# One of four low one-hot blocks of the expert stage moved from the vector engine to the scalar engine

## The chip, the cores and the metric

The kernel runs on one core of a Trainium2 chip. The metric is the device time of one execution in microseconds (us). Five instruction streams run side by side and meet only at semaphores: TensorE (PE, with its weight loads shown as PEld), VectorE (DVE), ScalarE (ACT), GpSimd (POOL) and SyncE (SP). Each runs its own instructions in the order in which they are written.

## The reference, cut to what matters

The network has four layers; the first three are left alone here. The last one is a product-key expert layer over 4 x 512 tokens of 128 numbers:

```python
q = (xn @ w_q.T).reshape(b, s, 2, NH, KD).transpose(2, 0, 1, 3, 4)
sim = jnp.einsum('pbnhd,hkpd->bpnhk', q, keys_p)          # 2 sides x 8 heads x 32 keys
scores, idx = jax.lax.top_k(sim, K)                        # K = 8 on each side
all_scores = scores[0][..., :, None] + scores[1][..., None, :]
all_idx = idx[0][..., :, None] * NK + idx[1][..., None, :] # NK = 32
sc, pk = jax.lax.top_k(all_scores, K)                      # 8 experts for each head
hmid = jax.nn.sigmoid(sc) * gelu(inputs . down[indices])
out = sum(hmid * up[indices])                              # over heads and k
```

So each token picks 64 experts (8 heads x 8) out of 1024 (32 x 32), with a weight for each.

## The kernel before

The first three layers are computed in the function layers(), the expert layer in peer(). It works on 16 tiles of 128 tokens, numbered u, in 8 **pairs** p of two tiles (256 tokens). Instead of gathering rows of down and up, it computes gelu(x . down) for all 1024 experts (hid) and multiplies it by a dense matrix of weights, which it builds from one-hots. An expert's number is split into a low part (0 to 127, the number modulo 128) and a high part (8 values). For every one of the 128 lanes (one token of either tile) TensorE multiplies a one-hot of the low parts (hot_lo, 128 chosen experts of the two tokens x 128 values) with the weighted one-hot of the high parts (hot_w), in two products (high and low half of the weight). The lanes are treated in QB = 4 **blocks** of LB = 32 lanes; block q has its own PSUM bank 2 + q.

The order in a pair is written out by hand on each engine, one loop over p from -1 to 7.

- VectorE, pair p: one_hots(p), which makes in_lo, w_lo, hi_t, lo_t, hot_hi, four hot_w and the four hot_lo blocks; residual(p - 1); second_choice of tiles 2p+2 and 2p+3, which ends in rc; normal(p - 1); which_side of both tiles, which writes eq from the rc that ScalarE has cast to 16 bits; weigh(p), which writes the four mix blocks, each once TensorE has filled its bank; first_choice of tiles 2p+4 and 2p+5.
- ScalarE, pair p: decoded(p), which brings the numbers of the chosen experts from PSUM (sides_t, w_hi, w_t) and so releases one_hots(p); side_numbers of two tiles (side_f); three hidden() (gelu of hid for the next 512 tokens); for even p normed() (xn); then in turn rows_columns(2p+2) (the cast of rc), key_scores(2p+4) (the copy keysims), rows_columns(2p+3), key_scores(2p+5); then sigmoids and one more hidden().
- TensorE, pair p: decoded(p); three hidden(); gathered(p), the 256 products of hot_lo and hot_w in four blocks, each behind hot_ok and its bank's mix_ok; key_scores(2p+4) and (2p+5), of which the second waits for ScalarE's copy of the first; one hidden(); outputs(p) behind the last mix.
- GpSimd: numbers(u) behind eq, candidates(u), root(p).

Pairs 0 to 5 have work for the next 512 tokens (hidden) and key scores; pairs 6 and 7 have neither.

Of the kernel before, what the change touches and what calls it, by code (L numbers as in the profile page):

```python
# [16 lines left out]
ALU = mybir.AluOpType  # L17
# [7 lines left out]
P = 128  # L25
# [1341 lines left out]
def peer(nc, v):  # L1367
# [5 lines left out]
    QB = P // LB  # L1373
# [10 lines left out]
    with ctx:  # L1384
# [19 lines left out]
        sides_t = sb("sides_t", [P, 2, P], U32)  # L1404
        w_t, w_hi, w_lo = sb("w_t", [P, P]), sb("w_hi", [P, P], F16), sb("w_lo", [P, P], F16)
        in_lo, lo_t, hi_t = sb("in_lo", [P, P], U32), sb("lo_t", [P, P], F16), sb("hi_t", [P, P], F16)
        hot_lo = sb("hot_lo", [P, P // 2, P, 2], F16)
        hot_hi = sb("hot_hi", [P, P // 2, EH, 2], F16)
        hot_w = sb("hot_w", [P, 2, P // 2, 2, EH, 2], F16)
# [10 lines left out]
        cand_ok, best_ok, rc_ok, rc16_ok = sem("cand_ok"), sem("best_ok"), sem("rc_ok"), sem("rc16_ok")  # L1420
        eq_is, eq_ok, sig_ok = sem("eq_is"), sem("eq_ok"), sem("sig_ok")
        dec_mm, dec_ok, split_ok = sem("dec_mm"), sem("dec_ok"), sem("split_ok")
        hot_ok, g_mm, mix_ok = sem("hot_ok", QB), sem("g_mm", QB), sem("mix_ok", QB)
        out_mm, z4_ok, var_ok, rstd_ok = sem("out4_mm"), sem("z4_ok"), sem("var4_ok"), sem("rstd4_ok")
        o4_ok, stored = sem("o4_ok"), (sem("stored0", 16), sem("stored1", 16))
        own = sem("dve_own4", 0)
# [1 line left out]
        with nc.Block() as block:  # L1428
# [52 lines left out]
            @block.scalar  # L1481
            def _(act):
                def normed(b):

                    if b:
                        wait(act, ksim_mm, T * b - 1)
                    nc.scalar.activation(xn[:], v.x3t[:, N * b:N * b + N], ACT.Identity, bias=bn_shift[:],
                                         scale=v.bn_scale[:]).then_inc(xn_ok.h, 1)

                def key_scores(u):  # L1490

                    wait(act, ksim_mm, u)
                    if u >= 4:
                        wait(act, found_ok, u - 4)
                    nc.scalar.copy(keysims[:, u % 4].rearrange("p s k -> p (s k)"), bank[6][:]).then_inc(ksim_ok.h, 1)  # L1495

                def hidden(b, c):

                    if b >= 2:
                        wait(act, mix_ok, PB * (b - 1) - 1)  # L1500
                    wait(act, h_mm, b, c + 1)
                    nc.scalar.activation(hid[:, b % 2, :, c, :], bank[H_BANK(b, c)][:].rearrange("p (t l) -> p t l", t=T),  # L1502
                                         ACT.Gelu).then_inc(h_ok.h, 1)

                def side_numbers(u):

                    wait(act, found_ok, u)
                    if u >= 4:
                        wait(act, eq_ok, u - 4)
                    nc.scalar.copy(side_f[:, u % 4].rearrange("p i r h -> p i h r"),  # L1510
                                   side_i[:, u % 4].rearrange("p (i h) r -> p i h r", i=2)).then_inc(side_f_ok.h, 1)

                def rows_columns(u):

                    wait(act, rc_ok, u)
                    if u >= 2:
                        wait(act, eq_is, u - 2)
                    nc.scalar.copy(rc16[:, u % 2], rc[:, u % 2]).then_inc(rc16_ok.h, 1)  # L1518

                def sigmoids(u):  # L1520

                    wait(act, best_ok, u)
                    if u >= 2:
                        wait(act, dec_mm, u // 2 - 1)
                    nc.scalar.activation(weight[:, u % 2], best[:, u % 2], ACT.Sigmoid).then_inc(sig_ok.h, 1)

                def decoded(p):

                    wait(act, dec_mm, p)
                    if p:  # L1530
                        wait(act, split_ok, p - 1)
                        wait(act, g_mm, p - 1)
                    nc.scalar.copy(sides_t[:].rearrange("p i l -> p (i l)"), bank[1][:, 0:2 * P])
                    nc.scalar.mul(w_hi[:], bank[1][:, 2 * P:3 * P], WEIGHT_SCALE)
                    nc.scalar.copy(w_t[:], bank[1][:, 2 * P:3 * P]).then_inc(dec_ok.h, 1)

                nc.scalar.copy(ident_h[:], ident[:]).then_inc(ident_ok.h, 1)
                act.wait_ge(bn_done.h, 1)
                normed(0)
                hidden(0, 0)  # L1540
                hidden(0, 1)
                for u in (0, 1):
                    key_scores(u)
                for c in range(2, EH):
                    hidden(0, c)
                for p in range(-1, PAIRS):
                    ahead = p >= 0 and p // PB + 1 < B
                    if p >= 0:
                        decoded(p)
                    if p + 1 < PAIRS:  # L1550
                        for u in (2 * p + 2, 2 * p + 3):
                            side_numbers(u)
                    if ahead:
                        for c in HID_EARLY[p % PB]:
                            hidden(p // PB + 1, c)
                    if p >= 0 and p + 2 < PAIRS and (p + 2) % PB == 0:
                        normed((p + 2) // PB)
                    for u in (2 * p + 2, 2 * p + 3):
                        if p < 0:
                            key_scores(u + 2)  # L1560
                        if u < TILES:
                            rows_columns(u)
                        if p >= 0 and u + 2 < TILES:
                            key_scores(u + 2)
                    if p + 1 < PAIRS:
                        for u in (2 * p + 2, 2 * p + 3):
                            sigmoids(u)
                    if ahead:
                        for c in HID_LATE[p % PB]:
                            hidden(p // PB + 1, c)  # L1570

            @block.vector
            def _(dve):
# [40 lines left out]
                def one_hots(p):  # L1614

                    wait(dve, dec_ok, p)
                    if p:
                        wait(dve, g_mm, p - 1)
                    nc.vector.tensor_scalar(in_lo[:], sides_t[:, 0], IN_LO - 1, None, ALU.bitwise_and)
                    step(nc.vector.scalar_tensor_tensor(w_lo[:], w_t[:], WEIGHT_SCALE, w_hi[:], ALU.mult, ALU.subtract))  # L1620
                    nc.vector.tensor_tensor(hi_t[:], sides_t[:, 0], in_lo[:], ALU.subtract)  # L1621
                    step(nc.vector.scalar_tensor_tensor(lo_t[:], in_lo[:], float(NK), sides_t[:, 1], ALU.mult, ALU.add))
                    step(nc.vector.tensor_tensor(  # L1623
                        hot_hi[:], bc(hi_t[:].rearrange("p (j s) -> p j s", s=2).unsqueeze(2), [P, P // 2, EH, 2]),
                        bc(iota_hi4[:].unsqueeze(1), [P, P // 2, EH, 2]), ALU.is_equal))
                    for t in range(2):
                        q = slice(HK * t, HK * t + HK)
                        for i, w in enumerate((w_hi, w_lo)):
                            ins = nc.vector.tensor_tensor(  # L1629
                                hot_w[q, i, :, t], hot_hi[q],  # L1630
                                bc(w[q].rearrange("p (j s) -> p j s", s=2).unsqueeze(2), [HK, P // 2, EH, 2]),
                                ALU.mult)
                    ins.then_inc(split_ok.h, 1)
                    for q in range(QB):
                        lanes, pairs = slice(LB * q, LB * q + LB), slice(LB // 2 * q, LB // 2 * (q + 1))
                        nc.vector.tensor_tensor(  # L1636
                            hot_lo[:, pairs],
                            bc(lo_t[:, lanes].rearrange("p (j s) -> p j s", s=2).unsqueeze(2), [P, LB // 2, P, 2]),
                            bc(v.iota_lo[:].unsqueeze(1), [P, LB // 2, P, 2]), ALU.is_equal).then_inc(hot_ok.h, 1)
# [78 lines left out]
            def _(pe):  # L1718
# [37 lines left out]
                def gathered(p):  # L1756

                    for q in range(QB):
                        wait(pe, hot_ok, p, q + 1)
                        if p:  # L1760
                            wait(pe, mix_ok, p - 1, q + 1)
                        for lane in range(LB * q, LB * q + LB):
                            for i in range(2):
                                c = 2 * EH * (lane % LB)
                                ins = nc.tensor.matmul(  # L1765
                                    bank[2 + q][:, c:c + 2 * EH], hot_lo[:, lane // 2, :, lane % 2],
                                    hot_w[:, i, lane // 2, :, :, lane % 2].rearrange("p t e -> p (t e)"),
                                    start=(i == 0), stop=(i == 1))
                        ins.then_inc(g_mm.h, 1)
# [63 lines left out]
```

## Time and profile before

| | |
|---|---|
| time, median of 3 runs | 667.36 us (666.91 to 669.09) |
| profiled execution, its time | 663.84 us |
| profiled execution, its span | 662.1 us |
| VectorE busy over the span | 526.0 us, 79% |
| TensorE busy | 433.0 us, 65% |
| ScalarE busy | 199.9 us, 30% |
| GpSimd busy | 197.5 us, 30% |
| expert stage | from about 374 us to the end at 662 us |

The engines' shares are means over stages with different limits; the expert stage is read apart below. All positions in time are from the start of the span of this one profiled execution, whose own time lies 3.5 us under the median.

### The profile page before, as it was taken

The page shows a single profiled execution, that of the slowest core. Times are in us where ns is not written, and L with a number is a line of the kernel's source. Part 1 is how long each engine was busy: PE and PEld are TensorE (multiplying, and loading weights), DVE is VectorE, ACT ScalarE, POOL GpSimd, SP SyncE. Part 2 cuts the span into 40 slices and gives each one's busy share as a digit, 9 for nine tenths or more (in the row PEclk, how much of TensorE's full clock was granted, in tenths as well). Part 3 has the DMA queues.
Part 4 walks back from the last instruction along what each step waited for, and adds up shares of the span by engine and source line. Part 5 has one row for each costly group of instructions (what it writes and reads, how often), then busy time and mean ns, then how long its engine had stood idle before and what let it go on. Part 6 is the DMA issues. An engine that isn't in the chain of part 4 may idle for free. (4 is left out here: it accounts for less than half of the span.)

```text
span 662.1 us, 12046 instructions
## 1 busy us (share of the span) xinstructions
PE 433.0 (65%) x4504; PEld 308.1 (47%) x4504; DVE 526.0 (79%) x2100; ACT 199.9 (30%) x348; POOL 197.5 (30%) x185
## 2 busy tenths in 40 slices
PE   3776477775767658785276546867677767774344
PEld 2562256643655337653165214544544444544344
DVE  1668588688676977768874499999999999999783
ACT  2210264304452054521452343323232323231100
POOL 4332215703166130751256331303030303030200
PEclk9979767597865978567765685665856675756566
DMA  5500000000000000000000000000000000000000
GB/s 140 155 1 0 0 2 1 1 1 0 1 1 1 1 0 1 2 1 0 0 2 1 0 1 1 1 2 10 1 10 2 9 1 9 2 9 1 9 2 16
DMA packets 12456, 6.69 MB, mean 10 GB/s; under 512 B 3182, under 2 KB 11758, under 8 KB 12398
## 3 DMA queue, kind: packets, MB, share of 16 engines
q1 hardware_dynamic: 10622, 4.34, 2.6%
q10 hardware_dynamic: 1776, 1.58, 0.9%
q8 instruction: 35, 0.57, 0.4%
q14 instruction: 23, 0.19, 0.1%
HBM read 4.87 MB, written 1.05 MB: 9 GB/s over the span
## 5 line engine op out<-in xcount | busy, mean ns | idle before, releaser
L1765 PE MATMUL psum<-hot_w,hot_lo 128*128 128x16 f16 x2048 | 59.8, 174 | 29.7 <-DVE hot_lo L1636 29.7
L1765 PEld LDWEIGHTS psum<-hot_w,hot_lo 128*128 128x128 f16 x2048 | 57.1, 104 | 40.2 <-DVE hot_lo L1636 39.5
L1636 DVE TENSOR_TENSOR hot_lo<-lo_t,iota_lo 128x4096 f16<-128x4096 f16 x32 | 71.2, 2285 | 0.3
L1778 PE MATMUL psum<-upw,mix 128*128 128x128 f32 x256 | 45.5, 359 | 27.0 <-DVE mix L1651 27.0
L1739 PE MATMUL psum<-x3t,down_t 128*128 128x512 f32 x64 | 47.5, 850 | 22.4 <-ACT hid L1502 19.6
L1778 PEld LDWEIGHTS psum<-upw,mix 128*128 128x128 f32 x256 | 43.9, 271 | 36.3 <-DVE mix L1651 36.3
L1182 PE MATMUL psum<-q_hi,k_t 32*128 32x128 f16 x256 | 42.6, 285 | 27.5 <-DVE feat L830 18.8
L557 POOL TENSOR_TENSOR s_lo<-masked,s_hi 128x512 f16<-128x512 f32 x32 | 36.2, 1165 | 67.7 <-ACT s_hi L431 67.7
L1454 POOL TENSOR_TENSOR eq<-eq,side_f 128x1024 f16<-128x1024 f16 x16 | 33.1, 2090 | 69.1 <-DVE eq L1610 69.1
L1462 POOL TENSOR_TENSOR rstd<-rstd,minus_half 128x2 f32<-128x2 f32 x8 | 5.6, 705 | 129.0 <-DVE rstd L1668 129.0
L1182 PEld LDWEIGHTS psum<-q_hi,k_t 32*128 32x128 f16 x256 | 28.0, 125 | 32.9 <-DVE feat L830 20.9
L1182 PE MATMUL psum<-q_lo,k_t 32*128 32x128 f16 x256 | 43.3, 290 | 0.0
L1588 DVE FIND_INDEX8 side_i<-side,keysims 128x8 uint32<-128x32 f32 x256 | 41.5, 185 | 0.0
L1118 PE MATMUL psum<-we,x1t 128*128 128x512 f32 x64 | 37.4, 731 | 3.5 <-DVE z L761 3.5
L557 POOL TENSOR_TENSOR s_lo<-feat,s_hi 128x512 f16<-128x512 f32 x32 | 36.0, 1159 | 10.1 <-ACT s_hi L431 10.1
L1726 PE MATMUL psum<-keysim,xn 128*128 128x512 f32 x32 | 29.0, 1004 | 11.2 <-ACT keysims L1495 9.8
L1739 PEld LDWEIGHTS psum<-x3t,down_t 128*128 128x128 f32 x64 | 14.0, 253 | 46.2 <-ACT hid L1502 34.6
L1518 ACT CAST rc<-rc 128x128 f16<-128x128 uint32 x16 | 4.8, 298 | 100.1 <-DVE rc L1604 100.1
L761 DVE SCALAR_TENSOR_TENSOR z<-psum,wexp,z 128x128 f32<-128x128 f32 x112 | 29.6, 342 | 0.0
L1584 DVE MAX8 side<-keysims 128x8 f32<-128x32 f32 x256 | 25.2, 176 | 4.7 <-ACT keysims L1495 4.7
L1182 PEld LDWEIGHTS psum<-q_lo,k_t 32*128 32x128 f16 x256 | 28.0, 128 | 0.0
L1502 ACT ACTIVATE hid<-psum 128x512 f32<-128x512 f32 x32 | 20.6, 648 | 24.4 <-PE psum L1739 24.3
(237 smaller groups left out, 1075.4 us busy)
## 6 DMA issues: line engine op xcount, KB each, us to landing
xall<-in_L_attn_x SPq DMA_DIRECT2D x4, 256.0 KB, 4.7
out<-o SPq DMA_DIRECT2D x8, 128.0 KB, 1.8
we<-in_L_ffn_We SPq DMA_DIRECT2D x1, 512.0 KB, 4.1
downn<-in_L_ffn_down SPq DMA_DIRECT2D x1, 512.0 KB, 6.0
upw<-in_L_ffn_up SPq DMA_DIRECT2D x1, 512.0 KB, 6.8
wh<-in_L_attn_W_h SPq DMA_DIRECT2D x1, 256.0 KB, 4.2
keysn<-in_L_ffn_keys_p ACTq DMA_DIRECT2D x1, 256.0 KB, 11.7
wqkv<-in_L_attn_w_qkv ACTq DMA_DIRECT2D x1, 192.0 KB
```

Of the source, the lines that this page charges most:

```text
L557: nc.gpsimd.tensor_tensor(s_lo[:, u % 2, g, :], masked[u % 2][:, g, :], s_hi[:, u % 2, g, :], ALU.subtract).then_inc(slo_ok.h, 1)
L761: ins = nc.vector.scalar_tensor_tensor(z2[:, u, :], src, wexp[:, u, e:e + 1], (z2 if e else x1)[:, u, :], ALU.mult, ALU.add)
L1118: ins = nc.tensor.matmul(bank[Y_BANK[u] + k][:], x1t[:, P * u:P * u + P], v.we[:, 4 * k:4 * k + 4, :].rearrange("p e m -> p (e m)"), start ...
L1182: ins = nc.tensor.matmul(bank[4 + g % 2][:, P * c:P * c + P], k_t[r, u, c, :], q[r, u, c, :], start=(q is q_hi), stop=(q is q_lo))
L1454: nc.gpsimd.tensor_tensor(hit, hit, bc(side_f[:, u % 4].rearrange("p i r h -> p (i r) h").unsqueeze(3), [P, 2 * K, NH, K]), ALU.mult)\
L1584: ins = nc.vector.max(side[:, u % 4, s, :], keysims[:, u % 4, s, :])
L1588: ins = nc.vector.max_index(side_i[:, u % 4, s, :], side[:, u % 4, s, :], keysims[:, u % 4, s, :])
L1636: nc.vector.tensor_tensor(hot_lo[:, pairs], bc(lo_t[:, lanes].rearrange("p (j s) -> p j s", s=2).unsqueeze(2), [P, LB // 2, P, 2]), bc(v.i ...
L1726: nc.tensor.matmul(bank[6][:], xn[:, P * (u % T):P * (u % T) + P], v.keysim[:].rearrange("p s k -> p (s k)"), start=True, stop=True)\
L1739: nc.tensor.matmul(bank[H_BANK(b, c)][:], v.down_t[:, c, :], v.x3t[:, N * b:N * b + N], start=True, stop=True).then_inc(h_mm.h, 1)
L1765: ins = nc.tensor.matmul(bank[2 + q][:, c:c + 2 * EH], hot_lo[:, lane // 2, :, lane % 2], hot_w[:, i, lane // 2, :, :, lane % 2].rearrange ...
L1778: ins = nc.tensor.matmul(bank[0][:, P * t:P * t + P], mix[:, EH * t + e, :], v.upw[:, e, :], start=(e == 0), stop=(e == EH - 1))
```

## The change

VectorE makes three of the four hot_lo blocks of a pair. The fourth (lanes 96 to 127) is made by ScalarE in a new function last_one_hots(p). VectorE first writes lo_last, the low numbers of those 32 lanes as 32-bit floats. ScalarE then writes, for each of the 32 lanes, the distance of the numbers 0 to 127 (iota_f) from the lane's low number, |iota - lo|, with the lane's column of lo_last as the bias of an Abs instruction, and at last max(1 - distance, 0) over the whole block of 4096 columns in place. TensorE's fourth block waits for hot_last_ok.

```diff
+        lo_last, iota_f = sb("lo_last", [P, LB]), sb("iota_f", [P, P])
...
-        hot_ok, g_mm, mix_ok = sem("hot_ok", QB), sem("g_mm", QB), sem("mix_ok", QB)
+        hot_ok, g_mm, mix_ok = sem("hot_ok", QB - 1), sem("g_mm", QB), sem("mix_ok", QB)
+        lo_last_ok, far_ok, hot_last_ok = sem("lo_last_ok"), sem("far_ok"), sem("hot_last_ok")
...
+                def last_one_hots(p):
+                    pairs = slice(LB // 2 * (QB - 1), LB // 2 * QB)
+                    act.wait_ge(lo_last_ok.h, p + 1)
+                    for lane in range(LB):
+                        ins = nc.scalar.activation(hot_lo[:, LB // 2 * (QB - 1) + lane // 2, :, lane % 2], iota_f[:],
+                                                   ACT.Abs, bias=lo_last[:, lane:lane + 1], scale=-1.0)
+                    ins.then_inc(far_ok.h, 1)
+                    act.wait_ge(far_ok.h, p + 1)
+                    nc.scalar.activation(hot_lo[:, pairs], hot_lo[:, pairs], ACT.Relu, bias=1.0, scale=-1.0)\
+                        .then_inc(hot_last_ok.h, 1)
...
+                nc.scalar.copy(iota_f[:], v.iota_lo[:, :, 0])
...
                     if ahead:
                         for c in HID_EARLY[p % PB]:
                             hidden(p // PB + 1, c)
+                    if p >= 0:
+                        last_one_hots(p)
                     if p >= 0 and p + 2 < PAIRS and (p + 2) % PB == 0:
                         normed((p + 2) // PB)
...
                     nc.vector.tensor_tensor(hi_t[:], sides_t[:, 0], in_lo[:], ALU.subtract)
+                    last = slice(LB * (QB - 1), LB * QB)
+                    nc.vector.scalar_tensor_tensor(lo_last[:], in_lo[:, last], float(NK), sides_t[:, 1, last], ALU.mult,
+                                                   ALU.add).then_inc(lo_last_ok.h, 1)
...
-                    for q in range(QB):
+                    for q in range(QB - 1):
...
                     for q in range(QB):
-                        wait(pe, hot_ok, p, q + 1)
+                        if q < QB - 1:
+                            wait(pe, hot_ok, p, q + 1)
+                        else:
+                            pe.wait_ge(hot_last_ok.h, p + 1)
+                            wait(pe, split_ok, p)
```

On ScalarE the instructions of pair 1, from the three gelu of hid to the second copy of key scores, stood like this before:

```order
L1502 ACTIVATE hid<-psum 128x4x128 [waits h_mm] x3
L1518 CAST rc<-rc 128x128 [waits eq_is,rc_ok]
L1495 COPY keysims<-psum 128x512 [waits found_ok,ksim_mm]
L1518 CAST rc<-rc 128x128 [waits eq_is,rc_ok]
L1495 COPY keysims<-psum 128x512 [waits found_ok,ksim_mm]
```

and stand like this now:

```order
L1505 ACTIVATE hid<-psum 128x4x128 [waits h_mm] x3
L1546 ACTIVATE hot_lo<-iota_f,lo_last 128x128 [waits lo_last_ok]
L1546 ACTIVATE hot_lo<-iota_f,lo_last 128x128 x31
L1550 ACTIVATE hot_lo<-hot_lo 128x4096 [waits far_ok]
L1521 CAST rc<-rc 128x128 [waits eq_is,rc_ok]
L1498 COPY keysims<-psum 128x512 [waits found_ok,ksim_mm]
L1521 CAST rc<-rc 128x128 [waits eq_is,rc_ok]
L1498 COPY keysims<-psum 128x512 [waits found_ok,ksim_mm]
```

The 33 new instructions stand between the gelus and the two casts of rc. No table load is added to ScalarE's stream in any pair.

On TensorE the fourth block of gathered and the key scores behind it stood like this before (the first of the two key scores waits for xn_ok, the second for ksim_ok of the first):

```order
L1765 MATMUL psum<-hot_w,hot_lo 128x16 [waits mix_ok,hot_ok]
L1765 MATMUL psum<-hot_w,hot_lo 128x16 x63
L1726 MATMUL psum<-keysim,xn 128x512 [waits ksim_ok,xn_ok] x2
L1739 MATMUL psum<-x3t,down_t 128x512 [waits h_ok]
L1778 MATMUL psum<-upw,mix 128x128 [waits z4_ok,mix_ok]
```

and stand like this now:

```order
L1791 MATMUL psum<-hot_w,hot_lo 128x16 [waits mix_ok,split_ok,hot_last_ok]
L1791 MATMUL psum<-hot_w,hot_lo 128x16 x63
L1748 MATMUL psum<-keysim,xn 128x512 [waits ksim_ok,xn_ok] x2
L1761 MATMUL psum<-x3t,down_t 128x512 [waits h_ok]
L1804 MATMUL psum<-upw,mix 128x128 [waits z4_ok,mix_ok]
```

TensorE's order is the same; the fourth block's wait is for ScalarE instead of VectorE.

## Rows read from the trace of the kernel before

**Rows 1.** The page, part 5: the hot_lo group.

```profile
L1636 DVE TENSOR_TENSOR hot_lo<-lo_t,iota_lo 128x4096 f16<-128x4096 f16 x32 | 71.2, 2285 | 0.3
```

**Rows 2.** Busy time of the engines, pair 3 and pair 6 (windows).

```profile
500.40:533.50 33.10, 24.11 (x317) 16.03 (x317) 32.64 (x177) 8.87 (x17) 6.99 (x5) 0.64 0.02 6
599.60:632.00 32.40, 14.38 (x305) 13.81 (x305) 24.35 (x80) 3.73 (x9) 4.85 (x3) 0.58 0.02 5
```

**Rows 3.** Timeline of VectorE, first instruction of pairs 0, 1, 2, 3, 7.

```profile
402.97 0.20 DVE L1619 TENSOR_SCALAR in_lo<-sides_t 128x128 uint32<-128x128 uint32 x1
434.18 0.21 DVE L1619 TENSOR_SCALAR in_lo<-sides_t 128x128 uint32<-128x128 uint32 x1
467.38 0.23 DVE L1619 TENSOR_SCALAR in_lo<-sides_t 128x128 uint32<-128x128 uint32 x1
500.45 0.20 DVE L1619 TENSOR_SCALAR in_lo<-sides_t 128x128 uint32<-128x128 uint32 x1
632.05 0.23 DVE L1619 TENSOR_SCALAR in_lo<-sides_t 128x128 uint32<-128x128 uint32 x1 [7.71 <-ACT w_t L1535]
```

**Rows 4.** Timeline of VectorE: hot_lo and eq of pair 3, mix of 0, 3, 7.

```profile
504.76 8.90 DVE L1636 TENSOR_TENSOR hot_lo<-lo_t,iota_lo 128x4096 f16<-128x4096 f16 x4
521.50 1.28 DVE L1610 TENSOR_TENSOR eq<-rc,iota_r 128x1024 f16<-128x1024 f16 x2
...
423.39 2.47 DVE L1651 SCALAR_TENSOR_TENSOR mix<-psum,hid 128x512 f32<-128x512 f32 x4
...
522.70 2.48 DVE L1651 SCALAR_TENSOR_TENSOR mix<-psum,hid 128x512 f32<-128x512 f32 x4
...
647.95 2.48 DVE L1651 SCALAR_TENSOR_TENSOR mix<-psum,hid 128x512 f32<-128x512 f32 x4
```

**Rows 5.** Timeline of ScalarE: third hid of pairs 0 to 3, xn behind it.

```profile
410.68 0.60 ACT L1502 ACTIVATE hid<-psum 128x512 f32<-128x512 f32 x1 [2.17 <-PE psum L1739]
411.17 0.81 ACT L1487 ACTIVATE xn<-x3t,bn_shift,bn_scale 128x512 f32<-128x512 f32 x1
...
440.40 0.60 ACT L1502 ACTIVATE hid<-psum 128x512 f32<-128x512 f32 x1 [2.17 <-PE psum L1739]
...
472.13 0.60 ACT L1502 ACTIVATE hid<-psum 128x512 f32<-128x512 f32 x1 [1.28 <-PE psum L1739]
...
506.26 0.60 ACT L1502 ACTIVATE hid<-psum 128x512 f32<-128x512 f32 x1 [2.22 <-PE psum L1739]
```

**Rows 6.** Timeline of ScalarE: casts and copies of pairs 3 and 0.

```profile
518.07 0.30 ACT L1518 CAST rc<-rc 128x128 f16<-128x128 uint32 x1 [11.21 <-DVE rc L1604]
518.27 0.58 ACT L1495 COPY keysims<-psum 128x512 f32<-128x512 f32 x1
...
420.06 0.59 ACT L1495 COPY keysims<-psum 128x512 f32<-128x512 f32 x1 [0.50 <-PE psum L1726]
```

**Rows 7.** Timeline of ScalarE: gates of layer 1; w_hi, w_t, side_f.

```profile
247.89 1.25 ACT L357 ACTIVATE gate_t<-psum,bh_gate 128x512 f32<-128x512 f32 x2
...
431.07 0.28 ACT L1534 ACTIVATE w_hi<-psum 128x128 f16<-128x128 f32 x1
431.24 0.27 ACT L1535 COPY w_t<-psum 128x128 f32<-128x128 f32 x1
431.38 0.77 ACT L1510 CAST side_f<-side_i 128x128 f16<-128x128 uint32 x1
```

**Rows 8.** Groups of ScalarE by form: the gates.

```profile
L357 ACT ACTIVATE gate_t<-psum,bh_gate 128x512 f32<-128x512 f32 x8 | 5.1, 679 | 2.5 <-PE psum L1034 2.5
```

**Rows 9.** Timeline of TensorE, pair 0: fourth block, first key scores.

```profile
416.24 1.87 PE L1765 MATMUL psum<-hot_w,hot_lo 128*128 128x16 f16 x64 [0.33 <-DVE hot_lo L1636]
417.97 2.05 PE L1726 MATMUL psum<-keysim,xn 128*128 128x512 f32 x2
```

**Rows 10.** Timeline of TensorE and ScalarE: from outputs of pair 1 to decoded of pair 2.

```profile
458.97 6.62 PE L1778 MATMUL psum<-upw,mix 128*128 128x128 f32 x32 [2.49 <-DVE mix L1651]
465.42 1.06 PE L1750 MATMUL psum<-ident_h,eq 128*128 128x128 f16 x16
...
467.07 0.27 ACT L1535 COPY w_t<-psum 128x128 f32<-128x128 f32 x1
```

## The prediction

> **What bounds the kernel now.** I read the page's groups first: the 32 hot_lo blocks are the costliest VectorE group at 2285 ns each, 71.2 us [rows 1]. The busy time by stretch comes next. In pair 3 VectorE is busy 32.64 of 33.10 us, and ScalarE only 8.87 [rows 2]. So in the inner pairs VectorE is the bound, and what is taken from it comes back in full, as long as nothing it waits for gets late. In the stretch of pair 6 it is busy 24.35 of 32.40 us; it waits at the end for outputs and decoded, but these start behind its last mix, so the path still runs through it.
>
> The question is thus not the share of ScalarE but what stands behind the new block there. Two things do: the casts of rc, without which VectorE can't make eq, and the copies keysims. ScalarE runs in order, and the slots are given by the timeline. I count from the first instruction of one_hots in a pair, T: 402.97, 434.18, 467.38, 500.45 for pairs 0 to 3 [rows 3]. VectorE starts mix at T + 20.42 in pair 0 and at T + 22.25 in pair 3 [rows 3, 4].
>
> **What it removes.** Four blocks take 8.90 us, so a block is worth (8.90 - 2.285) / 3 = 2.2 us [rows 1, 4]. lo_last is new: 32 columns, a small instruction beside the 128 columns of in_lo (0.20 us) [rows 3]; I take 0.1 us, with 0 and 0.3 as the bounds, 2.4 us over 8 pairs at most. Where VectorE stays the bound, a pair gains 2.1 us.
>
> **What it adds on ScalarE.** The trace has no Abs with a column as bias on 128 columns, so its price is bounded. What counts is the distance from start to start. With no column as operand, w_hi to w_t on 128 columns from PSUM is 0.17 us [rows 7]; the cast of rc, which reads SBUF as the new instruction does, is followed after 0.20 us [rows 6]. The price of a column: two gates with a bias column take 1.25 us together and 0.679 each, so 0.57 from start to start [rows 7, 8]; hid, as wide but without one, is followed after 0.49 [rows 5]. That is 0.08 more. I take 0.20 + 0.08 = **0.28 us**, built from the nearest rows. The bounds: 0.17, if column and SBUF cost nothing, and 0.38 (0.30 of rc plus 0.08), if the instructions don't overlap.
>
> The last Abs must end before the Relu starts, 0.10 us. The Relu: 128 columns take 0.28 us [rows 7] and 512 take 0.60 [rows 5], 0.83 ns a column, so 4096 take 0.60 + 3584 x 0.83 ns = 3.58. The whole block is 32 x 0.28 + 0.10 + 3.58 = **12.64 us**.
>
> The Trainium skill gives another price for the 32 (ScalarE: Activation LUTs, section What ACT_TABLE_LOAD costs): an ACTIVATE with a column as bias takes some 280 ns + 0.833 ns a column, of which neighbours overlap by 93 ns. That is 0.294 us for 128 columns, an estimate from its figures, and would make the block 13.1 us and my result 2.7 us longer.
>
> **When it starts and ends.** In pairs 0 to 5 it stands behind the third hid. The next instruction can start 0.49 us after that one did (xn in pair 0) [rows 5]. Counted from T that is 8.20, 6.71, 5.24 and 6.30 us in pairs 0 to 3 [rows 3, 5]; pairs 2 and 3 are the shortest and longest of the last four, and I take their mean 5.77 for all four. lo_last is there long before, within 1 us of T.
>
> **What waits for it.** At the block's end TensorE may start the fourth block (0.05 for the signal, as w_t's end to in_lo in pair 2 [rows 3, 10]). Its key scores follow 1.73 us after that start [rows 9], and ScalarE's copy of them starts 2.09 us after theirs [rows 6, 9]. Only behind that copy stands the cast of rc of the pair's second tile: it starts 0.49 later (spacing as of hid), takes 0.30 [rows 6], 0.05 for the signal, then the second eq, 0.60 until mix [rows 4]. Together 5.31 us. So this is a loop through three engines: the block, TensorE's fourth block and key scores, the copy, the cast, eq. Before, the fourth hot_lo was followed by 8 us of other VectorE work before eq, which hid all of it. The normed of even pairs goes in TensorE's 1.87 us.
>
> Mix then starts at T + start of the block + 12.64 + 5.31:
> - pair 0: 8.20 + 17.95 = 26.15 instead of 20.42: 5.7 us later
> - pair 1: 6.71 + 17.95 = 24.66 instead of 22.25: 2.4 later
> - pairs 2 to 5: 5.77 + 17.95 = 23.72 instead of 22.25: 1.5 later each, 5.9
> - pair 6: no hid and no key scores. The block runs from T + 0.9 to T + 13.6, before eq at T + 21.05 - 2.1 (eq by pair 3 [rows 3, 4]). Full gain, -2.1.
> - pair 7: the block ends at 632.05 + 0.9 + 12.64 = 645.6, TensorE at 647.5 with its 1.87 [rows 3, 9]. VectorE starts mix 2.1 us earlier, at 645.85, and the fourth mix 1.8 us later, at 647.65 [rows 4]. Just hidden: -2.1.
>
> What follows mix keeps its distance: first_choice on VectorE, beside it outputs, decoded and w_t. In pair 1 outputs took 6.62 us, and w_t ended 0.04 us before in_lo started [rows 3, 10], so even slow outputs just fit. GpSimd's numbers start earlier than outputs end.
>
> **The sum.** 5.7 + 2.4 + 5.9 - 4.2 = +9.8 us on 663.84, so 673.6. The median of before is 3.5 us over its profiled execution; on it the time is **677.2 us**.
>
> **The rivals.** About 0.3%, 2 us, is what a measurement can tell from no change.
> - *Faster: the loop closes in time.* At 0.17 us an Abs the block is 9.1 us and mix comes at T + start + 14.4: pair 0 is 2.2 late, pair 1 gains 1.1, pairs 2 to 5 some 1.9 each, pairs 6 and 7 4.2, in all -10.7, 656.7 us. Each 0.01 us of the Abs is 1.9 us of the kernel, so it decides from 0.23 us downwards. For it: w_hi to w_t [rows 7]; ScalarE is idle enough. Against: the gates show that a column costs. 0.12.
> - *No change:* an Abs at 0.22 to 0.24 us, the gain of some pairs eaten by the others: 667.4. 0.06.
> - *No overlap:* at 0.38 us the block is 15.7 us, six pairs lose 3.1 more each, and in pair 7 TensorE ends 2.9 after the fourth mix could start: +31, 699 us. For it: all new instructions read the same tile and write 2-byte values between each other's. Against: the gates overlap by 0.11. 0.10.
> - *The spread write is slow:* an Abs writes every second 2-byte value. side_f also writes spread values, 16 bytes apart, and takes 0.77 us for 128 columns instead of 0.30 [rows 6, 7]. At such a price (0.75 us) the block is 27.7 us, six pairs lose 15 more, pairs 6 and 7 some 20: about 790 us. Against: hot_lo's steps are 4 bytes. 0.03. The Trainium skill (SBUF — State Buffer, section Door 1: The DMA port swizzle) says that accesses pay only where fewer than two fall in one 16-byte line; four do so here, one for side_f, whose row agrees.
> - *As forecast,* 0.69.
>
> **The numbers.** The forecast's own range is an Abs of 0.25 to 0.32 us (-5.8 to +7.7 us), and if TensorE's slower clock makes every pair's hid as late as pair 1's, another 4 x 0.94 = 3.8. That is 671 to 689, and 669 to 690 with an edge to the cases beside it; it leaves out most of the fast rival and of the two slow ones, about 2 in 10. Faster 0.12, the same 0.06, slower 0.82.
>
> **What would show it.** Right: VectorE idles before the second eq or before mix in pairs 0 to 5, most in pair 0, released by ScalarE's rc; ScalarE's Abs start every 0.28 us; mix starts 23 to 26 us after in_lo in pairs 0 to 5 and 20 in pair 6; TensorE idles before its fourth block for hot_lo from ScalarE. Wrong: no VectorE idle time there, or Abs spaced by less than 0.23; a TensorE clock so low after the longer gap that hid comes later than 7 us after in_lo; table loads ahead of the Abs.

## The result, and the profile after

| | before | after |
|---|---|---|
| median time | 667.83 us (4 runs, 666.91 to 669.09) | 683.57 us (4 runs, 681.50 to 683.97) |
| ratio | 1 | 1.0222, 95% interval 1.0197 to 1.0247 |
| span of the profiled execution | 662.1 us | 682.2 us |
| first one_hots to the end | 259.1 us | 274.2 us |

The kernel is 15.7 us slower; forecast were 9.8, in a range of 669 to 690 us. The kernel before was profiled in an execution of 663.84 us, faster than any of its four timed ones. Of the 20.1 us between the two spans 5.0 lie ahead of the first one_hots, and all of these are there before ScalarE makes iota_f (at 377.59 in the kernel after), the one instruction that the change adds in that part. I therefore compare from the first in_lo to the end: 682.2 - 408.02 = 274.2 against 662.1 - 402.97 = 259.1, 15.1 us, which agrees with the medians.

The page of the kernel after, part 5, has four groups that answer to [rows 1] or show its consequence:

```profile
L1791 PE MATMUL psum<-hot_w,hot_lo 128*128 128x16 f16 x2048 | 59.9, 174 | 69.3 <-ACT hot_lo L1550 43.2
L1546 ACT ACTIVATE hot_lo<-iota_f,lo_last 128x128 f16<-128x128 f32 x256 | 76.0, 425 | 0.9 <-DVE lo_last L1642 0.9
L1658 DVE TENSOR_TENSOR hot_lo<-lo_t,iota_lo 128x4096 f16<-128x4096 f16 x24 | 53.6, 2287 | 0.3
L1629 DVE TENSOR_TENSOR eq<-rc,iota_r 128x1024 f16<-128x1024 f16 x16 | 10.9, 691 | 30.6 <-ACT rc L1521 30.6
```

VectorE has 17.6 us less of hot_lo (71.2 - 53.6) and sits idle 30.6 us before eq, for the cast of rc on ScalarE. Before, both eq of pair 3 ran back to back [rows 4]. Pair 4 in the busy times by stretch, and pair 6 (columns as in [rows 2]):

```profile
552.08:588.15 36.07, 22.54 (x317) 14.66 (x317) 30.68 (x176) 22.57 (x51) 6.71 (x5) 0.62 0.02 5
623.65:654.44 30.79, 14.81 (x305) 14.24 (x305) 22.26 (x81) 16.86 (x42) 4.84 (x3) 0.56 0.02 6
```

In pair 4 VectorE is 2 us less busy than in pair 3 of before, and the pair lasts 3 us longer. ScalarE is at 22.57 of 36.07 us, so it isn't full; it is late. Pair 4 on ScalarE's timeline, to be laid beside [rows 5, 6]:

```profile
558.42 0.60 ACT L1505 ACTIVATE hid<-psum 128x512 f32<-128x512 f32 x1 [2.22 <-PE psum L1761]
558.91 9.49 ACT L1546 ACTIVATE hot_lo<-iota_f,lo_last 128x128 f16<-128x128 f32 x32
568.44 3.62 ACT L1550 ACTIVATE hot_lo<-hot_lo 128x4096 f16<-128x4096 f16 x1
571.96 0.80 ACT L1490 ACTIVATE xn<-x3t,bn_shift,bn_scale 128x512 f32<-128x512 f32 x1
572.66 0.28 ACT L1521 CAST rc<-rc 128x128 f16<-128x128 uint32 x1
575.93 0.59 ACT L1498 COPY keysims<-psum 128x512 f32<-128x512 f32 x1 [2.98 <-PE psum L1748]
576.41 0.30 ACT L1521 CAST rc<-rc 128x128 f16<-128x128 uint32 x1
```

TensorE in the same pair:

```profile
563.25 1.88 PE L1791 MATMUL psum<-hot_w,hot_lo 128*128 128x16 f16 x64 [0.32 <-DVE hot_lo L1658]
572.11 1.88 PE L1791 MATMUL psum<-hot_w,hot_lo 128*128 128x16 f16 x64 [6.98 <-ACT hot_lo L1550]
573.84 2.06 PE L1748 MATMUL psum<-keysim,xn 128*128 128x512 f32 x2
```

And VectorE, which answers to [rows 3, 4]:

```profile
552.08 0.20 DVE L1638 TENSOR_SCALAR in_lo<-sides_t 128x128 uint32<-128x128 uint32 x1
572.98 0.69 DVE L1629 TENSOR_TENSOR eq<-rc,iota_r 128x1024 f16<-128x1024 f16 x1 [1.86 <-ACT rc L1521]
576.75 0.69 DVE L1629 TENSOR_TENSOR eq<-rc,iota_r 128x1024 f16<-128x1024 f16 x1 [3.07 <-ACT rc L1521]
577.35 2.48 DVE L1673 SCALAR_TENSOR_TENSOR mix<-psum,hid 128x512 f32<-128x512 f32 x4
```

Read the three together. ScalarE's block ends at 572.06 (568.44 + 3.62); TensorE starts its fourth block 0.05 us later, its key scores 1.73 us after that; ScalarE waits 2.98 us for them to copy, and only then casts the second rc, which VectorE has been waiting for. It is the loop of the prediction, in every one of the first six pairs.

All pairs, in us from the pair's in_lo, worked out from the timelines (in_lo to in_lo is the length of a pair; the last is to the end of the span):

```
pair                      0      1      2      3      4      5      6      7
before  length         31.21  33.20  33.07  33.04  33.04  33.07  32.45  30.05
        mix            20.42  22.26  22.28  22.25  22.26  22.29  22.27  15.90
after   first Abs       8.20   6.71   5.89   6.33   6.83   6.27   0.87   0.89
        Relu ends      21.34  19.86  19.04  19.47  19.98  19.41  14.03  14.04
        mix            26.63  25.16  24.33  24.77  25.27  24.70  20.17  13.81
        length         37.43  35.95  35.12  35.56  36.07  35.50  30.79  27.76
```

### The profile page after: what moved, and what is told of

Read it like the earlier page. It is cut to its first block and busy times, and to the rows that moved or that the text cites. A ratio compares the mean times of both kernels' runs of the same rounds, so it can differ in the third digit from the quotient of the medians.

```text
span 682.2 us, 12312 instructions
## 1 busy us (share of the span) xinstructions
PE 433.8 (64%) x4504; PEld 307.2 (45%) x4504; DVE 508.8 (75%) x2100; ACT 304.5 (45%) x613; POOL 195.8 (29%) x185
## 5 line engine op out<-in xcount | busy, mean ns | idle before, releaser
L1546 ACT ACTIVATE hot_lo<-iota_f,lo_last 128x128 f16<-128x128 f32 x256 | 76.0, 425 | 0.9 <-DVE lo_last L1642 0.9
L1761 PE MATMUL psum<-x3t,down_t 128*128 128x512 f32 x64 | 50.3, 896 | 27.3 <-ACT hid L1505 24.6
L1457 POOL TENSOR_TENSOR eq<-eq,side_f 128x1024 f16<-128x1024 f16 x16 | 31.5, 1971 | 90.8 <-DVE eq L1629 90.8
L1658 DVE TENSOR_TENSOR hot_lo<-lo_t,iota_lo 128x4096 f16<-128x4096 f16 x24 | 53.6, 2287 | 0.3
L1804 PEld LDWEIGHTS psum<-upw,mix 128*128 128x128 f32 x256 | 37.5, 233 | 14.1 <-DVE mix L1673 14.0
L1804 PE MATMUL psum<-upw,mix 128*128 128x128 f32 x256 | 37.6, 317 | 7.5 <-DVE mix L1673 7.5
L1118 PE MATMUL psum<-we,x1t 128*128 128x512 f32 x64 | 40.2, 777 | 2.5 <-DVE z L761 2.5
L1629 DVE TENSOR_TENSOR eq<-rc,iota_r 128x1024 f16<-128x1024 f16 x16 | 10.9, 691 | 30.6 <-ACT rc L1521 30.6
L1550 ACT ACTIVATE hot_lo<-hot_lo 128x4096 f16<-128x4096 f16 x8 | 28.9, 3617 | 0.3
```

The source lines that it names most:

```text
L1118: ins = nc.tensor.matmul(bank[Y_BANK[u] + k][:], x1t[:, P * u:P * u + P], v.we[:, 4 * k:4 * k + 4, :].rearrange("p e m -> p (e m)"), start ...
L1546: ins = nc.scalar.activation(hot_lo[:, LB // 2 * (QB - 1) + lane // 2, :, lane % 2], iota_f[:], ACT.Abs, bias=lo_last[:, lane:lane + 1], s ...
L1550: nc.scalar.activation(hot_lo[:, pairs], hot_lo[:, pairs], ACT.Relu, bias=1.0, scale=-1.0)\
L1658: nc.vector.tensor_tensor(hot_lo[:, pairs], bc(lo_t[:, lanes].rearrange("p (j s) -> p j s", s=2).unsqueeze(2), [P, LB // 2, P, 2]), bc(v.i ...
L1761: nc.tensor.matmul(bank[H_BANK(b, c)][:], v.down_t[:, c, :], v.x3t[:, N * b:N * b + N], start=True, stop=True).then_inc(h_mm.h, 1)
L1804: ins = nc.tensor.matmul(bank[0][:, P * t:P * t + P], mix[:, EH * t + e, :], v.upw[:, e, :], start=(e == 0), stop=(e == EH - 1))
```

## The experiments

Six are single ideas on the changed kernel, three more grew out of their results. T is the start of in_lo, as in the prediction. Ratios are against the kernel before, timed together with each experiment. In the edits "..." stands for lines left out.

**The casts ahead of the copies.** ScalarE only:

```diff
                     for u in (2 * p + 2, 2 * p + 3):
...
                         if u < TILES:
                             rows_columns(u)
+                    for u in (2 * p + 2, 2 * p + 3):
                         if p >= 0 and u + 2 < TILES:
                             key_scores(u + 2)
```

> One edit on the changed kernel: on ScalarE both casts of rc stand ahead of both copies of key scores, so the second cast no longer waits for TensorE's fourth block and key scores. Theory A (the loss is a loop: block, TensorE's fourth block and key scores, copy, cast, eq, mix): mix starts 1.2 us after the block's end instead of 5.3; the first copy is now late for first_choice by 0.9 us, so a pair of the first six takes some 32.3 us instead of 35.6, and the kernel 660 to 666 us. Theory B (the loss is ScalarE's load, or its traffic slowing the others, wherever the casts stand): no change, 680 us or more.

Measured: 665.52 us, ratio 0.9943 (0.9921 to 0.9964), as theory A has it. In pairs 0 to 5 mix starts 1.8 to 2.1 us after the Relu's end instead of 5.3. Theory A had 1.2 us; in the even pairs xn stands in between, and in the odd ones VectorE's own work ends last. The pairs take 35.81, 31.76, 32.96, 31.89, 32.96 and 31.89 us, and the kernel is 18 us shorter than the changed one. The larger part is TensorE's leg of the loop (3.2 to 3.5 us in each of the first six pairs, by the distance from the Relu's end to mix). In pairs 1 to 5 the block also starts earlier, at T + 5.1 to 5.3 instead of 5.9 to 6.8, since the hids come sooner. A part of both is lost again at the end of each pair, where VectorE now waits for w_t. This wait also makes pairs 2 and 4 longer than 3 and 5. Here are the first instructions of pairs 5 and 6, with the waits at the end of pairs 4 and 5:

```profile
573.75 0.23 DVE L1639 TENSOR_SCALAR in_lo<-sides_t 128x128 uint32<-128x128 uint32 x1 [1.56 <-ACT w_t L1538]
605.64 0.23 DVE L1639 TENSOR_SCALAR in_lo<-sides_t 128x128 uint32<-128x128 uint32 x1 [0.52 <-ACT w_t L1538]
```

The first copy of key scores comes at T + 22.26 in pairs 2 to 5 alike, and xn holds mix up by only 0.3 us. But outputs, behind which w_t comes, take 4.64 us in pair 4 at a mean granted TensorE clock of 0.80, and 3.73 us in pair 5 at 1.00.

**Abs in the gaps between the hids.** ScalarE only, in pairs 0 to 5; distances(p, first, n) makes the n Abs from lane number first of the block, and last_one_hots(p) keeps the Relu alone:

```diff
                         for c in HID_EARLY[p % PB]:
                             hidden(p // PB + 1, c)
+                            if c != HID_EARLY[p % PB][-1]:
+                                distances(p, done, 7)
+                                done += 7
                     if p >= 0:
+                        distances(p, done, LB - done)
```

> One edit on the changed kernel: in pairs 0 to 5, 7 Abs stand behind the first hid and 7 behind the second, in the 2.2 us in which ScalarE waits for TensorE there; 18 stay behind the third. Theory A (the block's end is on the path): the block ends 14 x 0.29 = 4.1 us earlier in six pairs, -24.5 us, 657 to 663 us. Theory B (load): no change, 680 us or more. If the Abs push the hids back, less is gained, down to 670.

Measured: 666.29 us, ratio 0.9960 (0.9946 to 0.9975). The block ends at T + 15.6 to 15.9 in pairs 1 to 5 instead of 19.0 to 20.0, near what was expected, but the time is 3 to 9 us over theory A's. It lies in the range left for hids pushed back; yet the third hid is at most 0.64 us later than in the changed kernel, so that is not the reason. Each of pairs 1 to 5 takes 32.97 or 32.98 us. The reason is in the timeline of pair 3, with all engines:

```profile
527.13 1.93 POOL L1457 TENSOR_TENSOR eq<-eq,side_f 128x1024 f16<-128x1024 f16 x1 [6.54 <-DVE eq L1638]
527.31 0.30 ACT L1521 CAST rc<-rc 128x128 f16<-128x128 uint32 x1
...
527.64 1.96 DVE L1638 TENSOR_TENSOR eq<-rc,iota_r 128x1024 f16<-128x1024 f16 x1 [0.66 <-ACT rc L1521]
...
529.53 0.68 DVE L1682 SCALAR_TENSOR_TENSOR mix<-psum,hid 128x512 f32<-128x512 f32 x1
```

The second eq starts 0.5 us into GpSimd's multiplication of the first one's result and takes 1.96 us instead of 0.68; it ends 0.54 us behind GpSimd. Together with 0.66 us of wait for its cast, which still stands behind TensorE's key scores and the copy, next to nothing of the 2.1 us is left. In the five pairs the second eq starts 0.49 to 0.78 us into the multiplication and takes 1.99 to 1.69 us; its end lies 0.54 or 0.55 us behind GpSimd's each time, so GpSimd's end sets it.

**The first key scores ahead of the fourth block.** On TensorE, and xn ahead of the Abs on ScalarE, without which TensorE would wait for xn:

```diff
                         else:
+                            if p + 2 < PAIRS:
+                                key_scores(2 * p + 4)
                             pe.wait_ge(hot_last_ok.h, p + 1)
...
-                        for u in (2 * p + 4, 2 * p + 5):
+                        for u in (2 * p + 4, 2 * p + 5) if p < 0 else (2 * p + 5,):
                             key_scores(u)
```

> Two moves on the changed kernel: TensorE does the first key scores of a pair ahead of its fourth block, and ScalarE makes xn ahead of the Abs, so that they can. The copy then finds its key scores done. Theory A (loop through TensorE): mix starts 1.65 us after the block's end instead of 5.3, and nothing of first_choice gets late: six pairs at about 31.5 us, 656 to 664 us in all, some 3 us under the kernel with the casts ahead. Theory B (load, or the block's end alone): 680 us or more.

Measured: 659.87 us, ratio 0.9872 (0.9852 to 0.9892). Mix starts 1.5 to 1.6 us after the Relu's end in pairs 0 to 4 (expected 1.65), and in pair 5 VectorE's own work ends last. ScalarE no longer waits between its two casts (pair 4):

```profile
551.83 3.62 ACT L1550 ACTIVATE hot_lo<-hot_lo 128x4096 f16<-128x4096 f16 x1
555.35 0.28 ACT L1521 CAST rc<-rc 128x128 f16<-128x128 uint32 x1
555.53 0.58 ACT L1498 COPY keysims<-psum 128x512 f32<-128x512 f32 x1
556.01 0.30 ACT L1521 CAST rc<-rc 128x128 f16<-128x128 uint32 x1
```

The pairs take 34.34, 30.96, 31.92, 31.53, 31.09 and 30.96 us. So the theory of a loop through TensorE holds, and 30.96 us is VectorE's own work in a pair with one block less (pairs 1 and 5, in which it waits for nobody).

**The block made, but unused.**

```diff
-                        ins = nc.scalar.activation(hot_lo[:, LB // 2 * (QB - 1) + lane // 2, :, lane % 2], iota_f[:],
+                        ins = nc.scalar.activation(spare[:, lane // 2, :, lane % 2], iota_f[:],
...
-                    nc.scalar.activation(hot_lo[:, pairs], hot_lo[:, pairs], ACT.Relu, bias=1.0, scale=-1.0)\
+                    nc.scalar.activation(spare[:], spare[:], ACT.Relu, bias=1.0, scale=-1.0)\
...
-                    for q in range(QB - 1):
+                    for q in range(QB):
...
-                        if q < QB - 1:
-                            wait(pe, hot_ok, p, q + 1)
-                        else:
-                            pe.wait_ge(hot_last_ok.h, p + 1)
-                            wait(pe, split_ok, p)
+                        wait(pe, hot_ok, p, q + 1)
```

> ScalarE does all of its 33 instructions but into a spare tile that nobody reads; VectorE makes all four blocks as before the change, and TensorE waits for VectorE alone. Theory A (the wait for the block is the loss): the casts still stand behind the block, which delays eq only in pair 0, by 2.6 us; with lo_last the kernel takes 669 to 673 us. Theory B (ScalarE's load or its writes slow the other engines): 680 us or more.

Measured: 680.16 us, ratio 1.0168 (1.0148 to 1.0188). By its numbers this is theory B's result, 7 us over the top of A's. But load on ScalarE would cost in every pair, and the first six pairs take 36.42, 33.16, 35.18, 33.16, 35.18 and 33.16 us: pairs 2 and 4 are 2.0 us longer than the odd ones. TensorE in pair 4 shows what differs:

```profile
560.40 1.88 PE L1788 MATMUL psum<-hot_w,hot_lo 128*128 128x16 f16 x64 [0.33 <-DVE hot_lo L1659]
566.82 2.08 PE L1749 MATMUL psum<-keysim,xn 128*128 128x512 f32 x2 [4.55 <-ACT xn L1491]
```

xn, which ScalarE makes in even pairs, stands behind the block, and TensorE's key scores wait 4.55 us for it: a second way from the block's end to the second cast of rc, which I had left out of theory A's number. (In pair 4 the second eq also met GpSimd's multiplication and took 1.74 us; 1.1 us of that pair's loss is this.)

**The same with xn first.** One edit more than in the run before:

```diff
+                    if p >= 0 and p + 2 < PAIRS and (p + 2) % PB == 0:
+                        normed((p + 2) // PB)
                     if p >= 0:
                         last_one_hots(p)
-                    if p >= 0 and p + 2 < PAIRS and (p + 2) % PB == 0:
-                        normed((p + 2) // PB)
```

> As the run with the unused block (VectorE makes all four blocks, nobody reads ScalarE's), with one more edit: ScalarE makes xn ahead of its Abs. That run's pairs 2 and 4 took 35.18 us and its odd pairs 33.16. Theory A2 (there the even pairs lost to xn behind the block, for which TensorE's key scores waited): pairs 2 and 4 fall to 33.2 us and pair 0 from 36.4 to some 34.4, so the kernel to 673 to 675 us. If ScalarE's load itself cost the 2 us, nothing moves: 680 us.

Measured: 671.90 us, ratio 1.0047 (1.0030 to 1.0065), 1.1 us under the range of theory A2 and within that of theory A above. Pairs 2 and 4 fall to 33.17 and 33.16 us, pair 0 to 34.34, as forecast. What is left is pair 0 (3.1 us over before) and lo_last (0.1 us a pair). So theory B is out: 33 more ScalarE instructions a pair, with their writes (here to another tile), cost the others next to nothing where nobody waits for them.

**No column as bias**, one run: `bias=lo_last[:, lane:lane + 1]` replaced by `bias=1.0`, so that the fourth block does not hold the lanes' one-hots.

> The changed kernel with the constant 1.0 as bias of the 32 Abs instead of each lane's column (ScalarE's numbers are then not the lanes' distances, so the fourth block is not the one-hots). Abs start to start: mine, from the gates against hid, is 0.08 less than the 0.292 us measured, so 0.21 us; if a column costs nothing, 0.29. At 0.21 the six pairs are 2.5 us shorter each and the kernel near 668 us; pairs 6 and 7 do not move.

Measured: 665.46 us in one run. ScalarE's 32 Abs of a pair:

```profile
546.79 6.54 ACT L1546 ACTIVATE hot_lo<-iota_f 128x128 f16<-128x128 f32 x32
```

6.54 us instead of 9.49, so a column costs (9.49 - 6.54) / 32 = 0.09 us, and 0.20 us are left from start to start. That is a little more than the 0.08 us that the gates gave. The kernel is 2.5 us under the 668 us expected. Pairs 1 to 5 stop at 33.0 to 33.1 us: in pairs 2, 3 and 5 the second eq is long (1.06 to 1.50 us) and ends 0.55 us behind GpSimd's multiplication, as in the run with the gaps; in 1 and 4 its cast comes late enough to avoid that wait.

**A dense write**, one run: each Abs writes 128 neighbours instead of every second place, in an order of columns that is not the one TensorE reads.

> The changed kernel with each Abs writing its 128 values side by side instead of to every second 2-byte place (the fourth block then has its columns in another order than TensorE reads them). If the spread write is free, as the rows of side_f against the 4-byte step let me expect, an Abs stays at 0.42 us and 0.29 us from start to start, and the kernel at 680 to 684 us. If the spread costs something, both fall, and with them 6 x 32 times the difference.

Measured: 683.77 us in one run. An Abs is shorter by itself, 387 ns against 425:

```profile
L1546 ACT ACTIVATE hot_lo<-iota_f,lo_last x256: 384/387/402, 416.7 to 664.0; 128x128 f16<-128x128 f32 x128
```

But from the first Abs to the Relu's end it is 13.11 us instead of 13.14, and from Abs to Abs 0.292 us in both. The spread write lengthens the part that the next instruction overlaps, not the distance between them. The rival of the slow write is out.

**Gaps, and casts ahead.** The first two edits together.

> 14 Abs in the gaps between the hids, and both casts of rc ahead of both copies, TensorE's order untouched. In the run with the gaps alone pairs 1 to 5 took 32.97 us, since the second eq took 1.96 us instead of 0.68: it started 1.3 us after the first, while GpSimd multiplied the first tile's eq. With both casts done early the two eq stand back to back again. Theory A3 (the two engines got into each other's way on SBUF): both eq together 1.28 us, pairs 1 to 5 at 30.96 us, 652 to 657 us. If the long eq had another cause, it stays near 2 us and the pairs near 33.

Measured: 653.60 us (6 runs, spread widely from 650.3 to 658.0), ratio 0.9773 (0.9737 to 0.9809). Pairs 1 to 5 take 30.95 to 30.98 us, and the two eq stand back to back in 1.29 us (pair 4):

```profile
552.97 1.29 DVE L1639 TENSOR_TENSOR eq<-rc,iota_r 128x1024 f16<-128x1024 f16 x2
```

The long eq thus comes from its meeting with GpSimd: the same instruction with the same operands is short again at another time.

**Gaps, and the key scores ahead.** The second and third edits together.

> Both cures together on the changed kernel: 14 Abs in the gaps between the hids, TensorE's first key scores ahead of its fourth block, xn ahead of the last Abs. Theory A: the block ends near T + 16 in six pairs, before VectorE wants eq at T + 18.96, so VectorE is the bound again with 2.1 us less to do: pairs 1 to 5 at 30.96 us, pair 0 near 30; the expert stage some 243 us instead of 249.5 with the key scores moved alone, the kernel 652 to 656 us. Theory B (something else in the block costs time too, such as its writes): no better than 659 us.

Measured: 651.65 us (5 runs, 651.23 to 653.64), ratio 0.9752 (0.9730 to 0.9774), 0.35 us under the range of theory A. Pairs 1 to 5: 31.28, 30.97, 30.96, 30.97, 30.97 us; pair 0: 30.25. Pair 4 of this run on ScalarE (read from its start, 531.17) and VectorE:

```profile
532.38 2.17 ACT L1544 ACTIVATE hot_lo<-iota_f,lo_last 128x128 f16<-128x128 f32 x7
534.70 0.60 ACT L1505 ACTIVATE hid<-psum 128x512 f32<-128x512 f32 x1 [0.15 <-PE psum L1770]
535.20 2.18 ACT L1544 ACTIVATE hot_lo<-iota_f,lo_last 128x128 f16<-128x128 f32 x7
537.52 0.60 ACT L1505 ACTIVATE hid<-psum 128x512 f32<-128x512 f32 x1
538.02 0.81 ACT L1490 ACTIVATE xn<-x3t,bn_shift,bn_scale 128x512 f32<-128x512 f32 x1
538.73 5.40 ACT L1544 ACTIVATE hot_lo<-iota_f,lo_last 128x128 f16<-128x128 f32 x18
544.16 3.62 ACT L1554 ACTIVATE hot_lo<-hot_lo 128x4096 f16<-128x4096 f16 x1
...
549.75 0.30 ACT L1521 CAST rc<-rc 128x128 f16<-128x128 uint32 x1 [1.30 <-DVE rc L1632]
```

```profile
550.15 1.29 DVE L1638 TENSOR_TENSOR eq<-rc,iota_r 128x1024 f16<-128x1024 f16 x2
551.35 2.48 DVE L1682 SCALAR_TENSOR_TENSOR mix<-psum,hid 128x512 f32<-128x512 f32 x4
```

The 14 Abs fill waits that ScalarE had anyway (2.22 us before the second and the third hid in pair 4 of the kernel after, 0.15 us and less here). The block ends before rc of the second tile exists: the cast waits for VectorE again, as before the change. This version beats both kernels, the one before by 17 us (669.06 us, timed together) and the one after by 32 (683.57 - 651.65).

## Why the prediction came out as it did

The direction, the loop and the pairs in which it bites were right. The loss was 15.7 us against 9.8, because two terms were too small: the length of the block (the price of an Abs) and, in pairs 2 to 5, its start.

- **What bounds, and what one block is worth:** right. With the waits cured, a pair costs VectorE 30.96 us instead of 33.04 to 33.07: 2.1 us, with lo_last at 0.1 (33.16 with lo_last and all four blocks, in the run with the unused block and xn first).
- **The loop:** right in each link. Relu's end to mix is 5.29 or 5.30 us in pairs 0 to 5, forecast 5.31. Cutting TensorE's leg out of it, or moving the block's end, each by itself turned the loss into a small gain.
- **The block's length:** 13.14 us, forecast 12.64. The term that was too small is the Abs. From the first to the Relu's start it was 9.52 us, forecast 9.06: 0.292 us from start to start, and a last one of 0.425 to its end. The price of the column, 0.08, should have been 0.09, and the 0.20 under it was right (the run without a column). The 0.10 until the Relu starts, for which the prediction gave no row, was 0.16 (0.425 - 0.292, and 0.03 more). The Relu took 3.62, forecast 3.58. Six pairs: 6 x 0.5 = 3.0 us.

The Trainium skill's figures (ScalarE: Activation LUTs, section What ACT_TABLE_LOAD costs), 280 ns + 0.833 ns a column less 93 ns, gave an estimate of 0.294 us from start to start; the trace agrees, with 0.292, and it was nearer than my 0.28.

- **The block's start:** forecast T + 5.77 as mean of pairs 2 to 5, measured 6.33 (5.89, 6.33, 6.83, 6.27): 4 x 0.56 = 2.2 us. I took the hids' times over from before. In the prediction this stood in the range alone, as 3.8 us if all were as late as pair 1's. In pair 4 ScalarE waits 2.22 us before each of the second and third hid, nearly as in pair 1 of before (2.16 and 2.17), where pair 2 of before had 1.27 and 1.28. The traces show TensorE's granted clock as the difference; the two matmuls of a hid in pair 2 of before, and in pair 4 after:

```profile
470.91 1.13 PE L1739 MATMUL psum<-x3t,down_t 128*128 128x512 f32 x2 [0.75 <-ACT hid L1502]
553.43 2.07 PE L1761 MATMUL psum<-x3t,down_t 128*128 128x512 f32 x2 [2.92 <-ACT hid L1505]
```

From T + 0.4 to T + 6.2 the granted clock was 1.00 (the level of 2.4 GHz) in pair 2 of before and 0.51 in pair 4 after, nearly all of it at the level of 1.2 GHz. Pairs 2 to 5 had 1.00, 0.63, 0.73 and 0.82 before, and 0.71, 0.63, 0.51 and 0.63 after. Ahead of pair 2 of before TensorE had been busy up to T, and the clock stayed at 1.00; ahead of pair 4 after it had ended its work 1.6 us before T, and the clock fell some 0.5 us after T. No run changed this gap alone, so the cause of the lower clock stays open.

- **Pairs 0 and 1:** mix 6.2 and 2.9 us later, forecast 5.7 and 2.4; both starts as forecast (8.20, 6.71), the rest is the block's length.
- **Pair 6:** mix at T + 20.17, as forecast. The pair gained 1.7 us instead of 2.1, as outputs took 6.30 us against 5.86.
- **Pair 7:** "just hidden" was just missed. TensorE's fourth block ended at T + 15.98 and outputs began at T + 16.76, 1.67 us earlier than before instead of 2.1. The pair gained 2.3 us all the same, with outputs of 5.85 us against 6.44. These shorter outputs were not forecast: that pair 7 came out near its number is luck.
- **The sum:** +14.0 for six pairs was +19.0 (lengths 6.2, 2.75, 2.05, 2.5, 3.0, 2.4), and -4.2 for the last two was -3.95. 3.0 and 2.2 make up the 5 us. With them the forecast would have been 15.0 us above before, and from the first one_hots to the end the traces have 15.1.
- **A sentence that held only by its cover:** "the normed of even pairs goes in TensorE's 1.87 us" is true while TensorE's fourth block is waited for there. In the run with the unused block xn itself was what TensorE waited for; having it first took 6.1 us out of pairs 0, 2 and 4 and 8.3 us out of the median.
- **The rivals:** the faster one would have needed an Abs of less than 0.23 us, and it took 0.292. The run with a constant bias reached 0.20 us and 665.46 us. A straight line between the two measured points (683.57 us at 0.292) puts the break-even near 0.21 us, an estimate; the forecast had 0.22 to 0.24, without the long eq, which I did not know of and which held the pairs of that run at 33.0 us. No overlap and slow writes are out.

## What to carry to other kernels

Work moved to an idle engine is put into a queue: ask what stands behind it there, who waits for that, and whether the moved work's own reader stands ahead of something that this queue waits for in turn; here ScalarE was busy for 63% of pair 4 and the change lost 15.7 us. The same instructions placed in the queue's existing waits, with what the reader owes back issued first, turned it into a gain of 17. If an experiment misses its theory's number, look at which repetitions moved: here every second pair did, and that named the second wait.

## What the runs showed of the hardware that I had not expected

- A VectorE is_equal of 128x1024 16-bit values with both inputs in SBUF takes 0.68 us alone, and 1.96 us when it starts 0.5 us into a GpSimd multiplication that reads SBUF too. In all ten such meetings of three runs (gaps alone, unused block, no column), with starts from 0.49 to 1.68 us into the multiplication, it ends 0.54 or 0.55 us behind GpSimd. Back to back ahead of GpSimd the two take 1.29 us, and it is GpSimd's first multiplication that takes 2.25 us instead of 1.93. The Trainium skill (SBUF — State Buffer, section Who interferes with whom) says that a VectorE instruction with two SBUF inputs and a GpSimd instruction that reads SBUF lock each other out. The trace agrees in that GpSimd's end sets VectorE's, though 0.54 us behind it is a little less than the 0.68 us that the instruction takes alone.
- A column as bias costs a ScalarE instruction of 128 columns 0.09 us of issue distance (9.49 against 6.54 us for 32).
- A write to every second 2-byte place adds 38 ns to such an instruction's duration (425 against 387 ns), and nothing to the distance to the next.
- The same code ahead of the expert stage differed by 5.0 us between the profiled executions of before and after. Among the ten profiled kernels that have the change, the first in_lo starts at 406.55 to 409.10, against 402.97 in the one profile of before, so spans of whole kernels would have misled where a pair's length did not.
